# Lookups of two blocks in one run, Gram strips of 64 samples in one run, layers behind both

## The reference

```python
e = jnp.stack([tbl_0[ids[:, 0]], ..., tbl_25[ids[:, 25]]], axis=1)
all_emb = jnp.concatenate([bottom_output[:, None, :], e], axis=1)      # 2048 x 27 x 128
gram = jnp.einsum('bfd,bgd->bfg', all_emb, all_emb)
z = gram[:, _TRIU_I, _TRIU_J]                                          # 351 products a sample
h = jnp.concatenate([z, r_bottom_output], axis=1)                      # 2048 x 479
h = jnp.maximum(h @ W_top1 + b_top1, 0.0)                              # 512 wide
h = jnp.maximum(h @ W_top2 + b_top2, 0.0)                              # 256 wide
y = h @ W_top3                                                         # one number a sample
```

## Time and profile before

| what | value |
|---|---|
| runs, us | 360.71, 358.92, 360.54; median 360.54 |
| profiled execution, first to last instruction | 357.7 us |
| its own time around that | not given by itself; the median stands 2.8 us above this span |
| TensorE busy | 334.8 us (94%) |
| VectorE busy | 267.5 us (75%) |
| ScalarE busy | 205.6 us (57%) |
| GpSimd busy | 254.7 us (71%) |
| granted TensorE clock | 1.000 in the whole span |

### The profile page before, as it was taken

The page is one execution under the profiler, slowest core; times in us unless marked ns, Lnnn a source line. Parts: engine busy times, 40 slices in busy tenths (PEclk is TensorE's granted clock), DMA queues, the critical chain, the costliest instruction groups (busy, mean ns, idle before and its releaser), DMA issues.

```text
span 357.7 us, 14104 instructions
## 1 busy us (share of the span) xinstructions
PE 334.8 (94%) x6020; PEld 295.8 (83%) x6020; DVE 267.5 (75%) x810; ACT 205.6 (57%) x336; POOL 254.7 (71%) x274
## 2 busy tenths in 40 slices
PE   0678989899999999999999999999999999999996
PEld 0677889798988988888888888889888888888885
DVE  1999999994868869598777978788696987732412
ACT  3585776232334774757757566849666578552232
POOL 4777777777777777777777777777777777777600
DMA  6657468332225855849567496657766394732200
GB/s 211 180 166 244 136 172 295 96 83 63 55 53 112 150 113 106 131 101 176 101 129 131 84 151 134 127 104 121 155 99 141 85 175 109 106 83 57 58 5 1
DMA packets 60013, 42.91 MB, mean 120 GB/s; under 512 B 48816, under 2 KB 51504, under 8 KB 59824
## 3 DMA queue, kind: packets, MB, share of 16 engines
q1 hardware_dynamic: 51216, 24.38, 33.2%
q0 software_dynamic: 8448, 17.32, 20.9%
q10 hardware_dynamic: 288, 0.33, 0.4%
HBM read 31.24 MB, written 0.01 MB: 87 GB/s over the span
## 4 chain that ended last, share of the span: by engine, by line
PE 53%; DVE 16%; POOL 12%; DMA 9%; issue 5%; ACT 2%; SPq 2%; ACTq 0%; DVEq 0%
PE hot_ps L458 18%; POOL X L406 12%; DVE onehot L682 11%; PE h_ps L490 8%; PE gram_ps L436 8%; PE xt_ps L458 7%; PE h_ps L535 5%; DMA ids_wide<-in_hot_ids_dram 4%; PE h_ps L487 3%; DVE tab L749 2%; DMA stage_sb<-in_hot_dram 2%; DMA X<-in_table_dram,rows_sb 2%; PE xt_ps L420 1%; DMA turned<-planes 1%; PE zt_ps L472 1%
## 5 line engine op out<-in xcount | busy, mean ns | idle before, releaser
L406 POOL DMA_INDIRECT X<-in_table_dram,rows_sb x264 | 253.3, 959 | 83.3 <-issue 78.9
L682 DVE TENSOR_SCALAR onehot<-ids_wide,row_value 128x256 fp32r<-128x256 int16 x665 | 206.2, 380 | 39.2 <-PE hot_ps L458 23.2
L458 PE MATMUL hot_ps<-onehot,tab 128*128 128x256 f32 x1072 | 149.5, 291 | 14.4 <-ACT tab L861 11.1
L458 PEld LDWEIGHTS hot_ps<-onehot,tab 128*128 128x128 f32 x1072 | 135.2, 193 | 17.8 <-issue 15.3
L658 ACT COPY XT<-turned 128x512 int16<-128x512 int16 x82 | 65.7, 883 | 8.6 <-DMA turned<-planes 8.6
L832 ACT COPY XT<-hot_ps 128x256 f32<-128x256 f32 x60 | 41.2, 686 | 50.4 <-PE hot_ps L458 50.2
L436 PEld LDWEIGHTS gram_ps<-XT 128*27 128x27 f32 x4096 | 40.6, 105 | 28.3 <-issue 18.1
L436 PE MATMUL gram_ps<-XT 128*27 128x26 f32 x4096 | 53.0, 190 | 4.4 <-DVE Z L690 3.3
L822 ACT COPY planes<-X 128x1024 int16<-128x1024 int16 x41 | 44.5, 1086 | 13.2 <-DMA X<-in_table_dram,rows_sb 13.2
L490 PE MATMUL h_ps<-stage_sb,w_sb 128*128 128x256 f32 (+3 forms) x192 | 44.2, 366 | 0.0
L458 PE MATMUL xt_ps<-onehot,tab 128*128 128x256 f32 x288 | 40.8, 288 | 0.0
(11 more groups left out here) (54 smaller groups left out, 134.9 us busy)
## 6 DMA issues: line engine op xcount, KB each, us to landing
ids_wide<-in_hot_ids_dram SPq DMA_DIRECT2D x14, 320.0 KB, 4.6
X<-in_table_dram,rows_sb POOLq DMA_INDIRECT x264
stage_sb<-in_hot_dram SPq DMA_DIRECT2D x15, 256.0 KB
stage_sb<-in_hot_dram SPq DMA_DIRECT2D x10, 192.0 KB
bottomT<-in_bottom_t_dram SPq DMA_DIRECT2D x8, 128.0 KB
w_sb<-in_w_dram SPq DMA_DIRECT2D x1, 1024.0 KB
turned<-planes SPq DMA_TRANSPOSE x41
w_sb<-in_w_dram SPq DMA_DIRECT2D x1, 512.0 KB, 9.3
```

Source lines behind the costliest of these rows:

```text
L406: pool.indirect_dma_start(X[:, n % RING, k, :], None, table, bass.IndirectOffsetOnAxis(idx[:, column:column + 1], 0)).then_inc(gathered[n ...
L458: mm = pe.matmul(hot_bank(i)[:, 0:WIDE], tab[u][:, part, D * c:D * (c + 1)], onehot[p % ONEHOTS][:, c - PIECE[u][h], :], start=(c == 0 and ...
L682: compared = dve.tensor_scalar(onehot[p % ONEHOTS][:, c - PIECE[u][h], :], ids_wide[:, u, :], row_value[:, c:c + 1], None, ALU.is_equal)
```

## The change

On TensorE alone, blocks 16 to 53 are no longer done one by one but in 19 pairs, by a new function `half_tile`: the lookup slices of both blocks, Gram of both (64 samples, 128 records), and then both blocks' `mlp`. The blocks before 16 and from 54 on are as before. No instruction of another engine is changed, added or moved, and no instruction of TensorE is added or removed. `transposes(...)` is not called in the pairs, since their units are turned by DMA; block 54 is still done by `step`.

```diff
+            def half_tile(b):
+
+                t, j = b // BLOCKS, b % BLOCKS
+                lookups(*slice_of(b))
+                lookups(*slice_of(b + 1))
+                gram(b)
+                gram(b + 1)
+                mlp(t, j)
+                mlp(t, j + 1)
+
             def last_blocks():
...
-            for b in range(LAST - 1):
+            for b in range(TURN_FROM):
                 step(b)
+            for b in range(TURN_FROM, LAST - 2, 2):
+                half_tile(b)
+            step(LAST - 2)
             last_blocks()
```

## The result

The change makes the kernel slower: 367.74 us (median of four runs, 367.54 to 370.86) against 360.02 us before (358.92 to 360.71); the ratio is 1.0226, with a 95% interval from 1.018 to 1.0272. The profiled span goes from 357.7 to 365.7 us. I had forecast 357.2 us.

What follows compares the result with a forecast made beforehand. TensorE was taken to set the pace, GpSimd's gathers close behind at 40.1 us for eight blocks; 38.5 us of work plus 2.2 of waits gave 40.7, block 54 3.3 us earlier, so 357.2 us; range 356.0 to 363.5.

Steps and rivals of the forecast that it cites:

- the price of a Gram run of 64 samples: TensorE's one Gram visit per half tile: 1.30 us, two 32-sample runs less one entry into the run.
- 1.33: Upper bound in us for TensorE's Gram run of 64 samples: 2 x 0.667, if it goes on as a pair does.
- dispatch: Rival: instructions come slower in longer TensorE runs, so a Gram run takes 1.7 us; 364 us in all, chance 0.06.
- VectorE waited 3.97 us ahead of line 752: VectorE's layer 3 in the odd tile's last block waits for the later layer 2: idle for 4.4 us.
- waited for one-hots: TensorE's lookups in the two half tiles after VectorE's idle time wait for late one-hot pieces: 2.2 us a pair of tiles.
- Gram of block 19: At the start of the paired blocks, TensorE's Gram waits until ScalarE has moved this block: 3.0 us.
- the neighbours' 0.19 us a visit: Each TensorE visit to Gram costs the records beside it 0.19 us; visits per half tile fall from four to one.
- the direct step from layers to lookups: New order on TensorE: extra cost taken as 0, between 0 and half of 0.19 us by the rows.
- The cap: Block 63's transposes can't start before 341.6 us, 2.7 us behind its last gather's issue: at most 3.3 us gained.

Runs made afterwards that it cites:

- e6: Changed kernel, but in half tiles holding both layers 2 the first layer 2 stands between lookups and Gram: 362.99 us, ratio 1.0081 to the kernel before.
- e8: Changed kernel with each block done as lookups, its 32 samples of Gram in one run, its layer: 356.24 us, ratio 0.9858 to the kernel before.
- e10: Per-block order of lookups, 32 samples of Gram in one run, layer, extended to blocks 8 to 15 and 54: 358.25 us, ratio 0.9949 to the kernel before.
- e12: Changed kernel with both blocks' lookups joined, then 32 samples of Gram, first layer, 32 samples, second layer: 358.12 us, ratio 0.9874 to the kernel before.
- e5: Changed kernel plus 256 unused Gram products (512 records) in one run at the end of TensorE's program: the added run took 12.3 us.
- e9: Changed kernel with each transposing DMA of the turns replaced by a plain DMA of the same 256 KB: 362.49 us in one execution.
- e7: Changed kernel with lookups, 32 samples of Gram, lookups, 32 samples of Gram, then both layers: 363.41 us, ratio 1.005 to the kernel before.
- e1 to e4: Four reorderings of lookups, Gram and layers in the changed kernel's half tiles, first run on one slow occasion: 607.74, 599.26, 596.68 and 603.70 us.
- e4: Changed kernel with lookups, 32 samples of Gram, layer for each block, on the slow occasion: 603.70 us, where the kernel before took 552.74.

## Why the prediction was wrong

**The step that failed is the price of a Gram run of 64 samples.** I took 1.30 us, two pairs of strips, from runs of 64 records that are 0.667 us long. Measured were 1.71 us at the least, 1.89 in the median and 2.14 in the mean of 19. That is (2.137 - 1.30) x 19 = 15.9 us against the forecast, of which 3.6 are gaps of 0.98, 2.10 and 0.52 us at the 65th record, where the second block is first read (the profile names the moved block for the first two, "issue" for the third). I had even bounded the run from above by 1.33: a pair's price twice. But the rows that I had end at 64 records, the last 31 of which are already the slower ones, and a limit that begins later can't be bounded by them. The rival "dispatch", with a run of 1.7 us and 364 us in all, was the mechanism; I gave it 0.06 because "nothing in the pair of strips points to such a growth". Two things did. The second strip of a pair took 0.32 us where the backlog alone would have given 0.24. And the price of 0.667 us was that of the cheapest runs: of the nine runs of 64 records in the trace of before, two took 0.80 and 0.73 us. This is the first of them:

```profile
328.02 0.87 PE L436 MATMUL gram_ps<-XT 128*27 128x26 f32 x64
```

The Trainium skill's queue of 64 entries ("TensorE: Matmul & The Clock Gate", table of specifications), cited there, agrees with the 33 records at 7 to 8 ns. It doesn't tell of the gaps that come later, and they are most of the cost.

**A wait I didn't price:** layer 2 of one tile directly behind that of another waits until VectorE has read the one PSUM tile: 2.51 us in place of 1.73, four times, 3.1 us. I had read that VectorE's layer 3 would wait for layer 2, but not that TensorE would then wait for layer 3. e6 took both away, and the ratio to the kernel before fell from 1.0226 to 1.0081.

**Right in kind, wrong in size:** VectorE waited 3.97 us ahead of line 752 (forecast 4.4), and TensorE then waited for one-hots. The profile puts only 1.9 us to these waits in the whole stretch, since it counts from the modelled ends. By the starts, the lookups behind the z transposes take 6.41 us on average in the changed kernel and 5.56 in e6, 4.2 us in five places, where I had 2.2 in each of four pairs. With 42.8 and 44.1 us for eight blocks in place of 40.7, VectorE has more time to refill its buffers; that this made the wait smaller is argued, not shown. Gram of block 19 waited 0.80 us, not 3.0: TensorE came to it later (126.68 us for block 18, not 125.8), and the move was done earlier (128.77, not 129.4). Gram of block 27 waited 1.91.

**Right:** the neighbours' 0.19 us a visit, together with nothing for the direct step from layers to lookups. A half tile's lookups and two quarters of layer 1 take 5.67 + 3.38 = 9.05 us, and the forecast's terms for them are 5.38 + 0.19 + 3.46 = 9.03. It was the sum that came right; the two prices weren't told apart.

**The cap was too low.** I had let the last gather take 2.7 us to land and so put the most that could be gained at 3.3 us. The change never came near it. But e8's median is 4.6 us below that of the kernel before, and e10's profiled span 4.6 us. In e10 block 63's transposes start 1.64 us behind the end of the last gather's issue (338.75):

```profile
340.39 0.66 PE L420 MATMUL xt_ps<-ident,X 128*128 128x128 f32 x4 [0.96 <-DMA X<-in_table_dram,rows_sb]
```

Summed for blocks 16 to 53: -3.3 us forecast, +15.9 for Gram, +3.1 for layer 2, -4.6 for one-hots that were not waited for (2.2 x 4 - 4.2), -3.0 for block 19, whose wait the Gram term now holds: 8.1 us, with 8.1 measured.

**Open:** what makes the gaps of 0.14 to 0.51 us in the long runs. That a long run costs more than its strips is shown by e6, e8 and e12; what delays it is not. e5 has no such gaps at its quiet end, and e9 keeps them without the transposing DMAs; the gathers' and ids' traffic was not taken away. Nor is it shown which queue the 7.2 us of e7 behind e8 come from.

## What to carry to other kernels

The price of a run of very short matmuls (here 7 to 8 ns apart at first) needn't grow in step with its length: 32 records took 0.35 us, 64 a mean of 0.77 to 0.85, 128 1.7 and more. Against it stands what each visit costs the neighbours, and the best of these three lengths was 64. Price a longer run only from a run of that length, and from the mean of many, not from the cheapest. Before joining two steps on one engine, follow the buffer between them the whole way round: the consumer that waits longer for its input also frees its buffer later, and the second step stands behind it.

## What the runs showed of the hardware

TensorE's instructions came in transfers of 16 KB, 256 instructions. In e5, with hardly any other DMA traffic (a share of 0.07 or less), a batch began 2.33 to 2.68 us behind the start of its transfer, and 3.45 to 3.73 us behind the batch before. The Gram matmuls used one up in 1.07 to 1.50 us and stood still for the rest.

On the occasion of e1 to e4 the kernel before took 553 us in place of 360. In e4's trace TensorE's Gram records waited for "issue" in 197 places, 133.3 us in all, at a mean granted clock of 0.841. So a time from one occasion can't be set against one from another: each comparison needs the kernel before beside it.
